# Attention step of a fused attention and feed-forward kernel: six key-projection matmuls move in front of the probability transposes, and the query and key transposes in front of the output projection

## The reference

```
h = shift_token(x);  q, k, v = split(h @ wqkv)            # 512 -> 3 x 512, 8 heads of 64
q = l2norm(q) * qs;  k = l2norm(k) * ksc;  q, k = rotary_xpos(q, k)
bk, bv = look_around(k), look_around(v)                    # this window of 256 and the one before
sim  = einsum(q * 8, bk), masked to 0 <= i - j <= 256;  attn = softmax(sim)
x = x + (attn @ bv) @ wo
h = layernorm(shift_token(x));  a, g = split(h @ w1 + b1);  x = x + (a * gelu(g)) @ w2 + b2
```

## Time and profile before

| | |
|---|---|
| median of 3 runs | 2930.35 us (2930.16 to 2932.86) |
| the profiled execution | 2932.76 us, of which the span of the core 2930.9 us |
| PE busy | 2884.4 us, 98% of the span |
| PEld, DVE, ACT, POOL busy | 86%, 71%, 46%, 46% |
| granted TensorE clock | 0.998 of full speed over the span |

### The profile page before, as it was taken

One profiled execution on the slowest core, in us unless ns is written; L12 is line 12 of the kernel. 1 busy time (PEld: TensorE's weight loads), 2 busy tenths in 40 slices (PEclk: granted clock), 3 DMA queues, 4 the chain that ended last, 5 costly groups with the idle time before them and its releaser, 6 DMA issues. The chain is left out here.

```text
span 2930.9 us, 53002 instructions
## 1 busy us (share of the span) xinstructions
PE 2884.4 (98%) x20256; PEld 2531.0 (86%) x20256; DVE 2075.9 (71%) x4135; ACT 1341.3 (46%) x2807; POOL 1337.9 (46%) x1406
## 2 busy tenths in 40 slices
PE   9999999999999999999999999999999999999999
PEld 7887888888889899999998887878888899999998
DVE  8977777777667666766657768777666766666765
ACT  7865656555553222222235555556564322222222
POOL 7757677776542211122205667776662222212221
PEclk9999999999999999999999999999999999999999
DMA  6753233322157677776683223332127677777775
GB/s 219 238 184 98 94 113 104 109 91 80 37 199 276 252 266 265 266 259 256 255 314 110 94 98 109 106 111 93 57 76 282 241 279 270 273 277 275 276 276 188
DMA packets 184480, 547.01 MB, mean 187 GB/s; under 512 B 26262, under 2 KB 82074, under 8 KB 161700
## 3 DMA queue, kind: packets, MB, share of 16 engines
q1 hardware_dynamic: 184084, 543.56, 52.1%
q10 hardware_dynamic: 144, 0.07, 0.0%
HBM read 447.11 MB, written 93.70 MB: 185 GB/s over the span
## 5 line engine op out<-in xcount | busy, mean ns | idle before, releaser
L1242 PE MATMUL quad<-fhT_f,slot_f 128*128 128x256 f32 (+1 forms) x2088 | 596.4, 286 | 0.2 <-DVE sums_f L2056 0.2
L1243 PE MATMUL quad<-fhT_f,slot_f 128*128 128x256 f32 (+1 forms) x2088 | 590.2, 283 | 0.0
L1244 PE MATMUL quad<-fhT_f,slot_f 128*128 128x256 f32 (+1 forms) x2088 | 589.9, 283 | 0.0
L1242 PEld LDWEIGHTS quad<-fhT_f,slot_f 128*128 128x128 f32 (+1 forms) x2088 | 392.7, 188 | 1.4 <-DVE sums_f L2056 0.8
L1243 PEld LDWEIGHTS quad<-fhT_f,slot_f 128*128 128x128 f32 (+1 forms) x2088 | 392.9, 188 | 0.0
L1244 PEld LDWEIGHTS quad<-fhT_f,slot_f 128*128 128x128 f32 (+1 forms) x2088 | 392.9, 188 | 0.0
L1661 ACT ACTIVATE gate_f_raw<-gate_f_raw,bias_f 128x512 f32<-128x512 f32 (+1 forms) x176 | 127.2, 722 | 576.9 <-DVE gate_f_raw L2079 576.9
L1529 ACT ACTIVATE lprob<-lprob,small 128x384 f32<-128x384 f32 (+2 forms) x512 | 288.5, 565 | 179.1 <-DVE small L1880 179.1
L2164 POOL TENSOR_SCALAR stats<-stats 128x1 f32<-128x1 f32 x64 | 43.5, 680 | 707.5 <-DVE stats L2019 706.8
L2281 POOL TENSOR_TENSOR turned_qk<-with_cos,with_sin 128x256 f32<-128x256 f32 x252 | 186.9, 763 | 337.0 <-DVE with_sin L1904 243.6
L996 PE MATMUL bank_pair<-wqkv_h,hT 128*128 128x512 f32 x992 | 318.6, 402 | 0.0
(11 more groups left out here) (296 smaller groups left out, 7349.4 us busy)
## 6 DMA issues: line engine op xcount, KB each, us to landing
slot_f<-parts SPq DMA_DIRECT2D x160, 1792.0 KB, 7.6
slot_f<-parts SPq DMA_DIRECT2D x16, 1190.0 KB, 5.2
s_in<-stream SPq DMA_DIRECT2D x128, 128.0 KB, 2.7
s_res<-stream SPq DMA_DIRECT2D x64, 256.0 KB, 2.8
stream<-a_out SPq DMA_DIRECT2D x64, 256.0 KB, 2.0
res_f<-stream SPq DMA_DIRECT2D x63, 256.0 KB, 7.3
h_in_f<-stream SPq DMA_DIRECT2D x112, 128.0 KB, 6.7
parts<-part_high SPq DMA_DIRECT2D x20, 512.0 KB, 2.6
```

The lines of the kernel that those rows point to most:

```text
L1242: e.matmul(bank[0:n, :], high, row_high, start=c == 0, stop=False)
L1243: e.matmul(bank[0:n, :], high, row_low, start=False, stop=False)
L1244: ins = e.matmul(bank[0:n, :], low, row_high, start=False, stop=c == 1)
```

## The change

The last six K projection matmuls of a tile move from behind the transposes of queries and keys to the ten in front of the probability transposes, and the transposes of queries and keys move from behind `project_out` to its front. No instruction is added or removed, on any engine.

```
-PROJECTED = ((0, 12, 20), (20, 30, 36))
+PROJECTED = ((0, 12, 20), (20, 36, 36))
...
+                    if d and 2 <= s <= TILES:
+                        turn_q(s - 1)
+                        turn_k(s - 1)
                     if d and ended and s not in (TILES - 1, TILES):
                         project_out(tail, 0)
                     if d and ended and s not in (TILES - 1, TILES + 1):
                         project_out(tail, 1)
-                    if d and 2 <= s <= TILES:
-                        turn_q(s - 1)
-                        turn_k(s - 1)
```

## The result

The changed kernel takes 2949.6 us (median of 4 runs, 2949.5 to 2949.68), the kernel before in the same comparison 2930.85 us. The ratio is 1.0061 with a 95% interval of 1.0048 to 1.0073: slower by 0.6%. The forecast was 2949 us.

A forecast was written before the change was run, and what follows sets the result against it. PE, busy for 98% of the span, was taken as the bound, so only its gaps could move the time. 29.1 - 8.3 - 1.4 - 0.8 = +18.6 us on 2930.35 gave 2949 us, with 2938 to 2957 for 8 in 10.

The forecast's parts named there:

- The new wait: Query transposes wait for ACT's copy behind the probability transposes: 0.58 us more with three key tiles; net +29.1 us over 56 steps.
- The mis-sized term: With two key tiles, 0.20 us from the end of ACT's copy to PE's restart, within the estimated 1.45 us.
- The seam that I let go: The six K projection matmuls now follow ten of their kind, so one 0.10 us seam per half step goes.
- The delays that go: Probability transposes no longer wait for DVE's last maximum: -8.3 us; these transposes run faster: -1.4; late keys go: -0.8.
- 26 x 0.05: Probability transposes that had waited took 0.05 us more than others; over 26 places this was forecast as -1.4 us.
- The ends: Steps 2 and 31: the keys' wait for POOL turns into a later wait, 0; step 32's scores already wait for DVE, 0.
- a sign of being wrong: New waits of L1090 (scores) or L1880 (DVE maxima), among the listed signs that would refute the forecast.
- A: At the new wait only the shown 0.34 us idle counts, so the cost is +2.9 to +8.5 us: 2933 to 2939; 14%.
- B: Between the two runs of transposes there is no wait, price 0, and the other gains stay: 2914 us; 4%.
- C: `a_out` late delays DVE's maxima of half 0, some 0.3 us more in each of 56 steps, +17: 2966 us; 8%.
- D: Clock falls after the 20 transposes; twelve output matmuls at half speed cost 2.74 us more a step: 3103 us; 1%.
- E: Gaps only change places because a ring through DVE sets the step, so nothing changes: 2930 us; 3%.

The follow-up runs named there:

- The doubled copy: ACT copies the pair turned first in half 1 twice: in the changed kernel 2998.16 us, ratio 1.0223; in the kernel before 2935.82 us, ratio 1.0011.
- the covers: Changed kernel with one, two or three K projection matmuls between probability transposes and transposes of queries and keys: ratios 1.0014, 0.9974, 0.9961 to the kernel before.
- cover_3: Changed kernel with the last three K projection matmuls between probability transposes and transposes of queries and keys: 2921.51 us, ratio 0.9961 to the kernel before.
- project_only: Kernel before with only the six K projection matmuls moved; transposes of queries and keys stay behind the output projection: 2955.78 us, ratio 1.0079.
- turns_only: Kernel before with only the transposes of queries and keys moved in front of the output projection: 2967.58 us, ratio 1.012.
- out_split: Changed kernel with half of the output projection in front of the transposes of queries and keys: 2923.98 us, ratio 0.9972 to the kernel before.

## Why the prediction was right, step by step

**The new wait.** Forecast 1.81 us from L1112 to L893 with three key tiles, read from step 31; measured 1.81 in every such step from 4 to 31. The doubled copy shows that it is ACT's copy, the covers show that it is a release time and not a cost of PE's own. With two key tiles I had estimated 1.45; it is 1.38. The mis-sized term is the 0.20 us from the copy's end to PE's restart: I had halved the 1.51 us of two copies, but they overlap in the drawing; one lasts 0.81 us and the restart comes 0.14 us behind it, so 0.64 + 0.60 + 0.14 = 1.38. The seam that I let go is right too: the half step is 12.03, forecast 12.06.

**The delays that go.** A step without a DVE delay went from 20.79 to 21.30 (+0.51, forecast +0.51), one with a delay from 21.21 to 21.30 (+0.09, where 0.51 - 0.34 - 0.05 = 0.12 was the forecast), a step with one key tile from 18.18 to 18.68. That the delays are given back is shown by cover_3, where the new wait is hidden: steps 3 to 30 of both layers are 9.8 us shorter than in the kernel before, against the 10.5 us forecast. Its ratio of 0.9961 is 11 us (7 to 16 by its interval), but 1.4 us of that are in the steps at the ends. (In the sum, 26 x 0.05 is 1.3 and not 1.4.) The whole comes to 17.4 us in the two attentions against 18.6 forecast. Steps 3 to 30 gave 1.8 us less than forecast, 0.6 of it in the eight steps with two key tiles and the rest a few hundredths in each step; the ends gave 0.6 more. So the forecast of 2949 us lies nearer to the measured 2949.6 than its terms deserve: by the traces the sum is 1.2 us too high, and the profiled execution was forecast at 2951.4 us and took 2949.67. That the medians differ by 18.75 us, almost exactly the 18.6, is luck.

**The ends.** I counted 0 for steps 2, 31 and 32. Steps 2 and 31 gained what they lost but for 0.2 to 0.3 and 0.07 us: the keys' wait for POOL turned into one for DVE before the next scores. Step 2 by time:

```profile
233.33 1.06 PE L893 MATMUL quad<-ident,turned_qk 128*128 128x128 f32 x8 [0.35 <-POOL turned_qk L2292]
...
236.06 0.98 PE L1090 MATMUL quad<-kT,qT 64*128 64x256 f32 x12 [1.08 <-DVE kT L1714]
```

Here the releaser is named as POOL, whose 1.04 us end at 233.22. But the first of ACT's two copies began at 232.80, took 0.38 us and ended at 233.18, and L893 starts 0.14 us behind that, as in all other steps; so ACT's copy explains this start too. I had given as a sign of being wrong that L1090 gains waits. It did, by 1.2 us in all, of which step 2 has the larger part and gives it back. Step 32 shows a wait that I had not listed, keys 0.72 us late from POOL:

```profile
841.72 0.63 PE L893 MATMUL quad<-ident,turned_qk 128*128 128x128 f32 x4 [0.36 <-ACT lprobT L1350]
...
843.07 0.66 PE L893 MATMUL quad<-ident,turned_qk 128*128 128x128 f32 x4 [0.72 <-POOL turned_qk L2292]
```

It makes step 32 longer by 0.74 us, and step 33, where PE then waits 0.54 instead of 1.25 us for DVE, shorter by 0.72. My 0 for step 32 came out only because the two cancel; neither was foreseen.

**The rivals.** A (only the idle column counts) falls: the idle column has 20.4 us, and two covering matmuls brought back 25 (1.0061 to 0.9974). B (no wait) falls by the new wait itself. C (`a_out` late) falls: with three key tiles it starts 1.36 us ahead of the next scores, even a little earlier than in the earlier trace rows, and the first maximum comes 0.83 us behind the scores, before 0.82. The narrow place was the step with one key tile. There it ends 0.21 us behind the start of the scores and 0.45 us ahead of the first maximum, which comes 0.66 us behind the scores as before:

```profile
399.78 0.69 DVE L1928 TENSOR_TENSOR a_out<-bank,s_res 128x512 f32<-128x512 f32 x1 [1.28 <-PE bank L899]
400.26 0.98 PE L1090 MATMUL quad<-kT,qT 64*128 64x256 f32 x12
400.92 0.42 DVE L1880 CUSTOM_DVE_ANT_0 lprob<-quad,far 128x256 f32<-128x256 f32 x1 [0.45 <-PE quad L1090]
```

D (the clock) falls with the granted clock of 1.00 in both attentions; project_only shows what its fall would have looked like. E (a ring) falls with turns_only, where the waits add.

## What to carry to other kernels

When an engine writes a buffer, another reads it and the first writes it again, put other work of the first between its two writes, for as long as it would wait: here 0.5 us, two or three matmuls, were enough, and a block of twelve was not needed. The best orders tried, cover_3 and out_split, are 0.3 to 0.4% faster than the kernel before. Before moving such a block, look whether the new order stands somewhere in the trace already, at the ends of a pipeline above all; it gives the price. And read a gap from start to start: the idle column left out 0.24 of 0.58 us here, and showed nothing at all of the quarter of a microsecond that was left with one matmul inside.

## What the runs showed of the hardware

A copy of 128x768 from PSUM that had waited for PE starts 0.85 us behind the first of twelve transposes, the same whether ACT had been idle for 1.41, 1.19 or 0.73 us. Where a pair has four or two transposes instead of six, its copy starts 0.64 or 0.42 us behind the first of them. From the end of the copy to PE's next transpose it takes 0.14 us, the same behind copies of 0.38, 0.60 and 0.81 us. Twenty transposes in a row with a wait of 0.34 us in them left the granted clock at 1.00. Behind waits of 2.02 and 1.96 us in project_only it was 0.50 for 3.4 us each time.
